# A GNN kernel on one core: GpSimd announces gathered rows by the group and waits for single slots

## What is computed

```python
# GIN, each of 3 layers
edge_emb = edge_attr @ conv_edge_w[l] + conv_edge_b[l]
msg = relu(h_in[src] + edge_emb)
agg = segment_sum(msg, dst, num_segments=N)
# GATv2, each of 3 layers
m = xl[src] + xr[dst] + e;  m = where(m > 0, m, 0.2 * m)
s = einsum('ehc,hc->eh', m, att)
ex = exp(s - segment_max(s, dst)[dst]);  alpha = ex / segment_sum(ex, dst)[dst]
out = segment_sum(xl[src] * alpha[:, :, None], dst)
```

## Time and profile before

| | before |
|---|---|
| median of 3 runs | 12084.69 us |
| profiled execution | 12083.72 us |
| its span | 12081.9 us |
| mean granted TensorE clock | 0.727 |
| PE busy | 7981.0 us (66%) |
| DVE busy | 5646.3 us (47%) |
| ACT busy | 3137.0 us (26%) |
| POOL busy | 4817.6 us (40%) |

### The profile page before, as it was taken

The page is one execution under the profiler, slowest core; times in us unless marked ns, Lnnn a source line. Parts: engine busy times, 40 slices in busy tenths (PEclk is TensorE's granted clock), DMA queues, the critical chain, the costliest instruction groups (busy, mean ns, idle before and its releaser), DMA issues.

```text
span 12081.9 us, 185984 instructions
## 1 busy us (share of the span) xinstructions
PE 7981.0 (66%) x44683; PEld 5712.2 (47%) x44684; DVE 5646.3 (47%) x15775; ACT 3137.0 (26%) x10374; POOL 4817.6 (40%) x5412
## 2 busy tenths in 40 slices
PE   6988899444554444444456777776777776777786
PEld 2444488333332223322335555555655554655564
DVE  6888801322222222222225555556555556555556
ACT  1000130111121111111114444444444444333333
POOL 0001100455546555455544444433444443444442
PEclk9999999666776666666666666666666676667766
DMA  1000186122221111111111211111212111211111
GB/s 34 16 33 38 44 329 221 51 63 62 66 58 51 45 46 45 44 45 46 44 39 53 54 54 53 52 52 49 56 53 55 53 53 48 57 54 54 54 53 45
DMA packets 501817, 732.17 MB, mean 61 GB/s; under 512 B 128746, under 2 KB 406593, under 8 KB 485012
## 3 DMA queue, kind: packets, MB, share of 16 engines
q1 hardware_dynamic: 350484, 414.14, 10.3%
q0 software_dynamic: 150528, 308.58, 9.8%
HBM read 597.78 MB, written 124.32 MB: 60 GB/s over the span
## 4 chain that ended last, share of the span: by engine, by line
PE 23%; another core or an unknown queue 16%; issue 12%; DVE 10%; DVEq 8%; ACT 1%; ACTq 0%; POOL 0%; DMA 0%; SPq 0%; POOLq 0%
PE ps L939 6%; PE ps L975 4%; PE ps L942 4%; PE ps L950 3%; PE ps L966 2%; PE ps L790 2%; DVEq L1209 2%; DVEq L1157 2%; DVE w L1341 2%; DVEq L1208 1%; PE ps L884 1%; DVE ps L1352 1%; DVE w L1212 1%; DVE rows_and_onehots L1032 1%
## 5 line engine op out<-in xcount | busy, mean ns | idle before, releaser
L541 POOL DMA_INDIRECT rows_and_onehots<-node_table,idx x4704 | 4536.8, 964 | 1542.4 <-issue 1502.9
L790 PE MATMUL ps<-rows_and_onehots,w 128*128 128x128 f32 x5280 | 1002.4, 351 | 2188.1 <-ACT w L662 1562.2
L790 PEld LDWEIGHTS ps<-rows_and_onehots,w 128*128 128x128 f32 x5280 | 928.0, 258 | 2779.1 <-issue 2740.4
L536 POOL COPY idx<-src_g 128x8 int32 (+1 forms) x594 | 113.2, 191 | 4270.9 <-DVE hr L1395 2255.6
L662 ACT ACTIVATE w<-w 128x512 f32<-128x512 f32 x663 | 417.4, 630 | 3554.3 <-DVE w L1212 3069.4
L939 PE MATMUL ps<-w_L_gnn_We,hr 128*128 128x512 f32 x1344 | 1180.8, 976 | 178.5 <-issue 107.8
L950 PE MATMUL ps<-hr,rows_and_onehots 128*128 128x132 f32 (+1 forms) x5280 | 1032.0, 351 | 126.7 <-issue 71.0
L1212 DVE TENSOR_TENSOR w<-rows_and_onehots,ps 128x512 f32<-128x512 f32 x663 | 455.9, 688 | 1352.7 <-issue 758.2
L942 PEld LDWEIGHTS ps<-xrb,w 128*128 128x128 bf16 x8064 | 765.8, 131 | 681.3 <-issue 681.3
L1341 DVE TENSOR_TENSOR w<-rows_and_onehots,ps 128x512 f32<-128x512 f32 x669 | 459.5, 687 | 1285.5 <-remote 1054.4
L975 PE MATMUL ps<-segrhs,rows_and_onehots 128*128 128x5 f32 (+1 forms) x5328 | 902.6, 293 | 180.6 <-issue 180.0
(11 more groups left out here) (223 smaller groups left out, 11826.4 us busy)
## 6 DMA issues: line engine op xcount, KB each, us to landing
w<-turned_onehots_bf SPq DMA_DIRECT2D x672, 128.0 KB
rows_and_onehots<-node_table,idx POOLq DMA_INDIRECT x4704
hr<-in_ea SPq DMA_DIRECT2D x672, 64.0 KB
w<-adjacency_turned SPq DMA_DIRECT2D x26, 1600.0 KB, 6.9
adjacency<-rows_and_onehots SPq DMA_DIRECT2D x25, 1600.0 KB, 5.2
w<-adjacency SPq DMA_DIRECT2D x25, 1600.0 KB, 11.7
rows_and_onehots<-adjacency_turned SPq DMA_DIRECT2D x24, 1600.0 KB, 7.0
turned_onehots_bf<-w SPq DMA_DIRECT2D x224, 128.0 KB
```

The costliest lines, as they stand in the source:

```text
L541: pool.indirect_dma_start(out=G[q][:, (i % CH) * D:(i % CH + 1) * D], out_offset=None, in_=table[:, :], in_offset=bass.IndirectOffsetOnAxi ...
L790: m = pe.matmul(bank(u % 2, P), rows[u][:, c * D:(c + 1) * D], OH[u][:, c * P:(c + 1) * P], start=(c == 0), stop=(c == CH - 1))
```

## The change

`announce` gets a part (0 or 1) and handles one group: it waits for that group's four gathers and adds 1 to `landed`. `fetch_groups(k)` now runs in this order: announce the first group of pair k-1; load two entries of `taken_i` (for the first and the second slot), raise each to at least 1; wait for the first slot; wait for the list and copy the next one; two gathers; announce the second group of pair k-1; two gathers; wait for the second slot; four gathers. For the very first pairs, which need no slot back, the waits are left out as before. `pairs_begun` is counted twice for each pair. The number of gathers, their sizes, the ring and all other engines' programs stay.

```diff
@@ -528,6 +528,7 @@
                 pool.wait_ge(bank_copied, PARTS * (t + 2))
                 pool.tensor_tensor(old, new, old, ALU.subtract).then_inc(tile_counted, 1)
 
+            taken, done = ([pool.alloc_register(f"{what}{part}") for part in range(2)] for what in ("taken", "done"))
             for S, name in zip(ALL, EDGES):
                 pool.wait_ge(stored, IN_TABLE[name])
 
@@ -535,35 +536,45 @@
 
                     pool.tensor_copy(idx8[slot][:, :], src_g[:, bass.ds(k * 2 * CH, 2 * CH)]).then_inc(S["listed"], 1)
 
-                def fetch_rows(slot, part, S=S):
-                    for i in range(part * CH, (part + 1) * CH):
-                        q = (2 * slot + part) % RING
+                def fetch_rows(slot, chunks, S=S):
+                    for i in chunks:
+                        q = (2 * slot + i // CH) % RING
                         pool.indirect_dma_start(
                             out=G[q][:, (i % CH) * D:(i % CH + 1) * D], out_offset=None, in_=table[:, :],
                             in_offset=bass.IndirectOffsetOnAxis(ap=idx8[slot][:, i:i + 1], axis=0),
                         ).then_inc(S["gathered"][q], 16)
 
-                def announce(k, slot, S=S):
-
-                    for part in range(2):
-                        q = (2 * slot + part) % RING
-                        pool.wait_ge(S["gathered"][q], (k * 2 + (part - q)) * (16 * CH // RING)
-                                     + (16 * CH + S["gathered before"][q]))
-                    pool.sem_inc(S["landed"], 2)
+                def announce(k, slot, part, S=S):
+
+                    q = (2 * slot + part) % RING
+                    pool.wait_ge(S["gathered"][q], (k * 2 + (part - q)) * (16 * CH // RING)
+                                 + (16 * CH + S["gathered before"][q]))
+                    pool.sem_inc(S["landed"], 1)
 
                 def fetch_groups(k, slot, S=S, list_rows=list_rows, fetch_rows=fetch_rows, announce=announce):
 
-                    if not (isinstance(k, int) and k < RING // 2):
-
-                        done = pool.value_load(taken_i[0:1, bass.ds(k * 2 + (1 - RING), 1)], min_val=1, max_val=STEPS)
-                        pool.wait_ge(S["weighted"] if "weighted" in S else S["summed"], done)
+                    given_back = S["weighted"] if "weighted" in S else S["summed"]
+                    reused = not (isinstance(k, int) and k < RING // 2)
+                    follows = not (isinstance(k, int) and k < 1)
+                    if follows:
+                        announce(k - 1, (slot - 1) % RING, 0)
+                    if reused:
+
+                        pool.reg_load(taken, taken_i[0:1, bass.ds(k * 2 - RING, 2)])
+                        for of, least in zip(taken, done):
+                            pool.reg_alu(least, of, 1, ALU.max)
+                        pool.wait_ge(given_back, pool.snap(done[0], min_val=1, max_val=STEPS))
                         pool.sem_inc(pairs_begun, 1)
                     pool.wait_ge(S["listed"], k + (1 + S["listed before"]))
                     list_rows(k + 1, (slot + 1) % RING)
-                    fetch_rows(slot, 0)
-                    if not (isinstance(k, int) and k < 1):
-                        announce(k - 1, (slot - 1) % RING)
-                    fetch_rows(slot, 1)
+                    fetch_rows(slot, range(0, 2))
+                    if follows:
+                        announce(k - 1, (slot - 1) % RING, 1)
+                    fetch_rows(slot, range(2, CH))
+                    if reused:
+                        pool.wait_ge(given_back, pool.snap(done[1], min_val=1, max_val=STEPS))
+                        pool.sem_inc(pairs_begun, 1)
+                    fetch_rows(slot, range(CH, 2 * CH))
 
                 pairs, fetch = GROUPS // 2, fetch_groups
                 peeled = RING + pairs % RING
@@ -574,7 +585,8 @@
                     for k in range(peeled, peeled + RING):
                         fetch(j * RING + k, k % RING)
                 pool.wait_ge(S["listed"], pairs + 1 + S["listed before"])
-                announce(pairs - 1, (pairs - 1) % RING)
+                for part in range(2):
+                    announce(pairs - 1, (pairs - 1) % RING, part)
 
         @block.scalar
         def _(act):
```

## The result

The changed kernel takes 11595.5 us (median of four runs, 11555.5 to 11603.0) beside 12079.7 us of the kernel before: a ratio of 0.9585, interval 0.9551 to 0.9618. The direction and the mechanism held; the size was three times too small.

The account below looks back on a forecast made before the run. It took a closed loop of GpSimd's gathers and VectorE, with PE's results held back while gathers run, as the bound. 12083.7 less 110 (GAT) and 50 (GIN 0) gave 11923.7, so 11925 us; range 11750 to 12210.

Parts of the forecast that it names:

- (a): GIN and GAT passes: announcing landed rows group by group and earlier gains 0, since VectorE hardly waits for announcements.
- the bound of 42: VectorE's add L1212 in GIN: 42.3 us over 30 waits on the announcing line, taken as the most earlier announcing could gain.
- (b): GpSimd's waits for landed rows moved ahead of slot waits and gathers: cost 0, bound 130 us.
- (c): Two-entry load, two register operations and one more semaphore increment per pair on GpSimd: cost 0, bound 170 us.
- (d): GAT passes: splitting the slot wait lets four gathers start a step earlier; 165 us computed, 110 us gain taken.
- the formula: GAT mean step: 42% merged pairs at 16.7 us, 58% single steps at 8.04 us, giving 8.22 against 8.50 us.
- the hold: PE's results reach VectorE late, from 2 to 3 us after a burst's first gather until about 2.6 after its last starts.
- (e): Split slot wait in GIN: runs of 12 gathers replace 16 in GIN 0, up to 100 us, 50 taken; GIN 1 and 2, 0.
- a third add in time: GIN 1 and 2: most cycles have a third add some 10 us into the burst, keeping groups back to back; gain 0.
- Merged bursts: Rival: the second slot is free in time, bursts of eight are rebuilt, only part of (e) stays; 12060 us, chance 0.25.
- The slower rival: GAT: small bursts each bring a hold; interval after a late first one passes 8.7 us; 12285 us, chance 0.20.
- The rule of the Trainium skill: DMA never contends with a compute engine: steps with and without gathers cost the same, change worth nothing, 12084 us.

Follow-up runs that it names:

- n1_announce: Changed kernel with one wait for both slots, announcements by group and early, against the kernel before, with the hold: 12117.4 against 12113.6 us, 0.9998.
- k1_changed: The changed kernel again, against the kernel before, without the hold: 8913.7 against 8949.9 us, 0.9966.
- m1_split: Changed kernel with announcements, still by group, back after the first four gathers; slot wait split. Against the kernel before, with the hold: 11604.6 against 12118.5 us, 0.9578.
- c1_changed: The changed kernel again, against the kernel before, with the hold: 11627.5 against 12126.8 us, 0.9586.
- k2_split: Same kernel as m1_split, against the kernel before, without the hold: 0.9946.
- e1_split_only: Same kernel as m1_split, against the kernel before, without the hold: 8898.8 against 8951.2 us, 0.9936.
- e2_announce_only: Same kernel as n1_announce, against the kernel before, without the hold: 0.9948.
- e3_gap4: Changed kernel, but no four gathers start before the four ahead have landed; against the kernel before, without the hold: 1.2475.
- n2_gap4: Same kernel as e3_gap4, against the kernel before, without the hold: 1.2502.
- p1_gap_in_pair: Changed kernel, but a pair's second four gathers wait until its first four landed; against the kernel before, without the hold: 9972.4 against 8955.7 us, 1.1144.

## Why the prediction was right and wrong

**(a) Announcements, 0: right in size; the bound of 42 rested on too little.** n1_announce, 0.9998. The row that gave 42.3 us counts only waits whose end is on record. In the trace of the kernel before 758.2 us of waits at L1212 (398 times) end at "issue", with no recorded end, where k1_changed has 76.7 (77 times), and of the 588 announcements 403 have a record of their increment (more on this at the end). So n1_announce decides it, not the row. The openings of the passes, which I hadn't foreseen, do get shorter by the announcement by the group: 5 us in each GIN pass in all three kernels that have it, and outside the six passes the changed kernel, m1_split and n1_announce are 25, 20 and 22 us under the kernel before. In n1_announce's total nothing of that is left; its interval reaches down to a gain of 16 us.

**(b) and (c), moved waits and register operations, 0: right as far as can be told.** n1_announce holds both together with (a); its interval bounds the three together by a gain of 16 us or a loss of 11, where 130 and 170 had been left for (b) and (c) alone.

**(d) The split wait in GAT, forecast 110, measured 315: the mechanism right, the step mis-sized.** To check the formula I cut each GAT pass, without its ends, at every weighing after which GpSimd started to gather again (more than 2.2 us after its last start), and counted gathers and weighings up to the next such release. Before, there are 279 of these cycles, all with eight gathers: the 213 pairs with two weighings, and 66 with three, in which one group straddles two tiles and so has a step of its own that frees no slot. The changed kernel has 347:

| | forecast | changed kernel |
|---|---|---|
| four gathers, one weighing | 58% at 8.04 us | 38% (106 of 277) at 7.98 us |
| eight gathers, two weighings | 42% at 16.7 us | 62% (171) at 16.33 us |
| mean step of these two kinds | 8.22 us | 8.12 us (8.51 before) |
| what a straddling group's extra step adds (66) | not priced (6.35 us before) | 4.87 us |
| interval after a late first one, if it starts with a release | 7.0 us | 5.8 us (about 105) |

The two prices of the formula held: a merged pair whose first interval is under 6.0 us takes 16.51 us (146 of them), a late single step 7.98. Three other things failed. First, I had marked the term down from 165 to 110 for the second four gathers, whose hold "opens sooner", and there was nothing to mark down: 5.8 us after a late first interval is below every value that I had weighed. That is 55 us. Second, the mean of the ordinary steps is 0.1 us lower than forecast, among other things because 25 of the merged pairs came from a first interval of 6.0 us or just over and took 15.26 us; over 588 groups that is some 60 us, although more cycles merged than the 42% taken. Third, the formula has no place for the 66 extra steps of straddling groups, which it silently took as unchanged. Each adds 4.87 instead of 6.35 us: 98 us, the largest single piece. 110 + 55 + 60 + 98 = 323, beside 315 measured. The other two traces with the split wait and the hold repeat this: ordinary steps 8.09 and 8.12 us, extra steps 5.11 and 4.82 (c1_changed, m1_split), where n1_announce has 8.54 and 6.43.

Why the extra step became cheaper isn't settled: no run takes it apart. The granted clock of the GAT passes rose with it, 0.68 before, 0.73 in the changed kernel, 0.71 in m1_split with the same gain (means of the levels 1.2 and 2.4 GHz), and no run separates the two.

**(e) GIN 0, forecast 50, measured 85; GIN 1 and 2, forecast 0, measured 23 and 43.** One cycle of the changed kernel in GIN 0, beside the earlier trace rows:
```profile
2447.31 0.97 POOL L542 DMA_INDIRECT rows_and_onehots<-node_table,idx  x1 [0.47 <-issue]
...
2461.27 0.95 POOL L542 DMA_INDIRECT rows_and_onehots<-node_table,idx  x1 [0.30 <-issue]
2466.22 0.95 POOL L542 DMA_INDIRECT rows_and_onehots<-node_table,idx  x1 [4.00 <-DVE w L1224]
...
2464.75 0.69 DVE L1224 TENSOR_TENSOR w<-rows_and_onehots,ps 128x512 f32<-128x512 f32 x1 [2.66 <-remote]
```
The last of twelve gathers starts at 2461.27, and the next run 18.9 us after the first one of this: 6.3 us a group, the low end of the forecast (19.0 and 6.3), with 4.0 us of idle where 6.87 stood. In GIN 0, 50 of 71 unbroken runs of gathers (starts at most 1.8 us apart) have this form, where 35 of 59 had sixteen before. The cycle was right and the discount of its 100 us to 50 was not. In GIN 1 and 2 the reason for 0, a third add in time, doesn't hold in all cycles: runs of twelve appear there too (15 and 12, beside 24 and 27 of sixteen).

**The rivals.** Merged bursts were half true: of 559 groups in the cut GAT passes 417 still travel in runs of eight or twelve, and such a pair costs nearly what it did. But merging doesn't rebuild the old cycle, since the late steps between are now released singly. The slower rival is refuted at the point that it named: the interval after a late first one had to pass 8.7 us, and it is 5.8 (6.4 over all of some 150, also where no new run starts). The rule of the Trainium skill, SBUF — State Buffer, section Who interferes with whom, that DMA does not contend with a compute engine, had been taken to give 12084; with the hold the result speaks against what I drew from it. Without the hold the trace agrees with it in GAT: 5.05 us a step with gathers, 5.00 without.

**The range** ended at 11750 because it allowed (d) 165 us and (e) 100, nothing for GIN 1 and 2, and 70 over. Measured were 315, 85, 66 and 25 for the openings, 491 in all. The 150 us of (d) over its upper end and the 66 of GIN 1 and 2 are what carried the time out of it. That the direction came out is no luck, since m1_split and n1_announce bear the cause out.

## What to carry to other kernels

Where a producer waits for two slots at once in a closed loop with its consumer, split the wait before touching the announcements: the waits of the profile name the side that is late (GpSimd 2255.6 us for slots, VectorE 42.3 us for announcements), and here only the late side paid. Look at how much of the waiting ends at "issue" before you take a small row as a bound. Count what a finer release does over the whole loop, with every kind of step in the mean, the odd ones too: one step in nine gave nearly a third of the gain in GAT. And measure a small edit only beside the kernel before in the same comparison: here the same pair of programs differs by 4.1% or by 0.3%.

## What the runs showed of the hardware

That the hold comes and goes as a whole was unexpected. Three marks tell the two levels apart in a trace.

The first is PE's increments. For every matmul that raises a semaphore I took the time from its recorded end to the next recorded increment of that semaphore, where this comes before the next such matmul ends. Within 1.3 us after the start of a gather the median is 2.2 us in the kernel before (3105 matmuls), 1.5 in the changed one, in c1_changed and in m1_split, and 2.2 in n1_announce; 54 to 59% are over 1 us late, and the median of those is 4.2 to 5.2 us. With no gather running it is 0.01 us. In the traces without the hold (looked at: k1_changed, k2_split, e1_split_only, e2_announce_only, e3_gap4, n2_gap4, p1_gap_in_pair) it is 0.01 us always. The recorded increments of VectorE and ScalarE come 0.01 us after the end at both levels, so it is PE's that are late. The waiting engine bears it out: VectorE's mean idle time before the add L1341 is 3.87 us when gathers run as it begins and 0.49 otherwise, and 0.20 and 0.11 in k1_changed.

The second is the sequencers. 1090 of SyncE's 9112 register instructions (FUSED_REGOPS, MOVE, ALU_OP) in the kernel before, and 1020 in the changed one, take 0.6 us or more, and of VectorE's 14579 it is 469 and 451. In the fifteen traces without the hold none does.

The third is what the trace itself lacks. The 4704 gathers raise their semaphores 75264 times, 16 each. The five traces with the hold have a record of 15125 to 16730 of these increments, those of the same gathers without it 73114 to 74067. Of VectorE's own increments while gathers run the trace of the kernel before lacks 2715 of 5576, of PE's 732 of 3837. The programs ran through, so the increments took place and only their records are missing. It means that with the hold no landing time of a gather can be read, that many waits end at "issue" because what ended them isn't on record, and that counts of late increments are rough. Whether the loss is another effect of what makes the hold, or has a part in it, no run shows.

The gathers' own packets don't lengthen: those of 4096 bytes take 221 ns in the kernel before and in the changed one, 228 in k1_changed (medians). So it isn't the transfers that are slow. Whether PE's matmuls end late or only their increments come late the traces don't tell, since a matmul's recorded end is modelled; when its result can be used is told by the increment, or by the start of who waits for it.

What switches it stays open. The chip doesn't (chip 6 had both), nor the kernel (the changed kernel, the split alone, the announcements alone and the kernel before are each there at both levels). All four comparisons with the hold were of one new kernel, but so were two of the six without it.
